# Adding arrays of sums in the order in which they are loaded, and skipping result rows that do not count

## The reference

```
h = tokens + attention(layernorm(tokens))
x = layernorm(h)                                   # 1184 x 256
topidx, tw = 6 of 32 experts for each token, with weights
routed = sum over the 6 chosen e of  tw[e] * down_e(silu(x @ gate_e) * (x @ up_e))
shared = silu(x @ shared_gate) * (x @ shared_up) @ shared_down
anchor = anchor_l(x)  with one of 16 small experts l, chosen by the first expert
return h + routed + shared + 0.1 * anchor
```

## Time and profile before

| what | value |
|---|---|
| median of 3 runs | 388.85 us |
| profiled execution | 390.52 us |
| its span | 388.7 us |
| TensorE busy | 350.9 us (90%) |
| VectorE busy | 256.1 us (66%) |
| GpSimd busy | 188.7 us (49%) |
| ScalarE busy | 168.9 us (43%) |
| moved by DMA | 86.62 MB, of it 25.51 MB by the software queue |
| read from HBM, written | 50.72 MB, 35.35 MB |

### The profile page before, as it was taken

How to read it: one execution, slowest core, us unless ns; L and a number is a source line. 1 busy time by engine, 2 the same in 40 slices (tenths; PEclk the granted TensorE clock), 3 DMA queues, 4 the chain that set the end, 5 groups by cost and what they waited for, 6 DMA issues and landing times.

```text
span 388.7 us, 8177 instructions
## 1 busy us (share of the span) xinstructions
PE 350.9 (90%) x2566; PEld 300.0 (77%) x2566; DVE 256.1 (66%) x1091; ACT 168.9 (43%) x433; POOL 188.7 (49%) x206
## 2 busy tenths in 40 slices
PE   5899999989999897776899999999999999997494
PEld 3687787968869777565689999999999999985231
DVE  3447588988979968588665555555555555555394
ACT  1124135253244522432166433347777777775001
POOL 5000000175572753723777777777665666655400
PEclk9899999999999989699999999999999999999879
DMA  7899998133159531349997776767788886499944
GB/s 232 245 356 329 284 422 365 47 103 103 60 159 389 191 106 31 119 119 406 317 268 234 225 215 205 210 205 216 208 239 247 253 239 209 141 312 332 309 131 130
DMA packets 39836, 86.62 MB, mean 223 GB/s; under 512 B 6513, under 2 KB 30185, under 8 KB 38745
## 3 DMA queue, kind: packets, MB, share of 16 engines
q1 hardware_dynamic: 29856, 59.84, 49.6%
q0 software_dynamic: 9072, 25.51, 19.0%
q10 hardware_dynamic: 864, 0.73, 0.7%
HBM read 50.72 MB, written 35.35 MB: 221 GB/s over the span
## 4 chain that ended last, share of the span: by engine, by line
PE 62%; DMA 15%; DVE 13%; ACT 4%; issue 2%; SPq 2%; DVEq 0%
PE B L854 19%; PE B L872 9%; DMA W<-sums_d 8%; PE B L545 5%; PE B L835 5%; PE B L580 4%; PE B L892 4%; DMA e_sb<-rows_d 4%; PE B L663 3%; DMA W<-in_wg 2%; PE B L629 2%; PE B L649 2%; DMA rows_d<-spent,slot 1%; PE B L687 1%; DVE stats L1083 1%
## 5 line engine op out<-in xcount | busy, mean ns | idle before, releaser
L508 POOL DMA_INDIRECT rows_d<-spent,slot x77 | 74.8, 972 | 124.9 <-DVE slot L1293 103.3
L529 POOL DMA_INDIRECT sums_d<-spent,to_row x60 | 58.3, 971 | 30.7 <-DVE spent L1534 24.0
L872 PE MATMUL B<-W,e_sb 128*128 (+1 forms) x224 | 67.8, 384 | 3.8 <-DVE e_sb L1542 3.6
L1542 DVE TENSOR_TENSOR e_sb<-e_sb,B 128x128 f32<-128x128 f32 (+1 forms) x112 | 32.2, 288 | 57.7 <-ACT e_sb L1036 56.7
L854 PEld LDWEIGHTS B<-e_sb,UPW 128*128 128x128 f32 x476 | 62.6, 191 | 4.2 <-issue 0.9
L854 PE MATMUL B<-e_sb,UPW 128*128 128x128 f32 x476 | 63.8, 275 | 0.0
L529 POOL DMA_INDIRECT sums_d<-Y_own,to_row x52 | 50.5, 972 | 21.2 <-DVE Y_own L1534 13.0
L1036 ACT ACTIVATE e_sb<-B 128x128 f32<-128x128 f32 (+1 forms) x112 | 30.9, 276 | 48.0 <-PE B L854 45.4
L854 PEld LDWEIGHTS B<-e_sb,W 128*128 128x128 f32 x320 | 43.1, 191 | 2.8 <-ACT e_sb L1031 0.5
L854 PE MATMUL B<-e_sb,W 128*128 128x128 f32 x320 | 43.6, 275 | 0.2 <-ACT e_sb L1031 0.2
L1031 ACT COPY e_sb<-B 128x256 f32<-128x256 f32 x112 | 41.2, 369 | 5.4 <-PE B L835 5.4
(11 more groups left out here) (193 smaller groups left out, 526.3 us busy)
## 6 DMA issues: line engine op xcount, KB each, us to landing
e_sb<-rows_d SPq DMA_DIRECT2D x96, 161.0 KB, 3.0
W<-sums_d SPq DMA_DIRECT2D x7, 1232.0 KB, 17.1
rows_d<-spent SPq DMA_DIRECT2D x1, 7728.0 KB, 33.8
W<-in_wx SPq DMA_DIRECT2D x1, 6643.0 KB, 48.9
W<-in_wx SPq DMA_DIRECT2D x10, 516.5 KB, 8.5
W<-in_wx SPq DMA_DIRECT2D x1, 4576.0 KB, 17.1
W<-in_pt SPq DMA_DIRECT2D x4, 666.0 KB, 7.2
spent<-rows_d SPq DMA_DIRECT2D x16, 161.0 KB
```

What stands on the lines that cost most here:

```text
L508: pool.indirect_dma_start(rows_d, bass.IndirectOffsetOnAxis(ap=slot[0:n, t, j:j + 1], axis=0), xrow[0:n, t, :], None).then_inc(done, 16)
L529: pool.indirect_dma_start(sums_d, bass.IndirectOffsetOnAxis(ap=to_row[:, i:i + 1], axis=0), result(i), None).then_inc(y_sent[i % NY], 16)
L872: pe.matmul(B[6 + i % 2][:, 0:D], hid[:, i % 2, :], weights, start=True, stop=True).then_inc(D_ps, 1)
L1542: dve.tensor_tensor(out[0:n, i % 2, :], S[0:n, i % 2, :], ups, ALU.mult).then_inc(H_ok, 1)
```

## The change

Two edits. The two adding engines take the seven arrays in the order 1, 2, ..., 6, 0, where they took 6, 5, ..., 0. And each send carries an upper bound for its row numbers, `SPARE_ROW - 1`; rows with a larger number are to be left out and not to be an error. The bound is passed in a register that is set ahead of every send.

```diff
+IN_ORDER = list(range(1, CHOICES)) + [0]
...
                 pool.indirect_dma_start(sums_d, bass.IndirectOffsetOnAxis(ap=to_row[:, i:i + 1], axis=0),
-                                        result(i), None).then_inc(y_sent[i % NY], 16)
+                                        result(i), None, bounds_check=SPARE_ROW - 1,
+                                        oob_is_err=False).then_inc(y_sent[i % NY], 16)
...
             pe.wait_ge(hs_ok, NB)
-            for c in range(CHOICES, -1, -1):
+            for c in [CHOICES] + IN_ORDER:
...
-            for c in range(CHOICES - 1, -1, -1):
+            for n, c in enumerate(IN_ORDER):
                 dve.wait_ge(fin_ld[c], 16)
                 for q, (lo, hi) in enumerate(ON_DVE):
-                    if c < CHOICES - 1:
-                        dve.wait_ge(fin_dve, len(ON_DVE) * (CHOICES - 2 - c) + q + 1)
+                    if n:
+                        dve.wait_ge(fin_dve, len(ON_DVE) * (n - 1) + q + 1)
```

## The result

The changed kernel takes **384.25 us** (median of 4 runs, 383.96 to 385.69), where the kernel before took 389.88 beside it: a ratio of **0.986 (95% interval 0.983 to 0.990)**, some 5.3 us less. (The ratios are taken over the fast runs of both kernels alone, and so are not quite the quotients of the medians.) A second measurement of the same kernel, further down, gave 0.989 (0.984 to 0.994). So the change makes the kernel faster, inside the range, but by half of the 10.6 us of the forecast. The profiled execution took 383.96 us, with a span of 382.2.

What follows compares the result with a forecast made beforehand. Adding waited for the sixth load, and sends held back by loads delayed the lists. Lists ending at 359.2, 14.1 us of adding, copy and stores gave a 378.1 span, 10.6 us less: 388.85 - 10.6 = 378.3 us, range 376.5 to 386.

Steps and rivals of the forecast that it cites:

- Rival A: Tail of the lists: bytes go, but a send's completion still waits behind the loads; 6.2 us less, 382.6; chance 0.12.
- rival B: Sends: skipped rows are not skipped on the wire, so the tail stays; 5.1 us less, 383.8; chance 0.08.
- Part 1, the order: Adding on both engines: starts when the lists end, not at the sixth load; VectorE 14.12 us, TensorE 13.9.
- What is late next: Loads after reordering: the sixth array is covered; the seventh lands 6.6 us after the last send lands.
- Part 2, the skipped rows: Sends beside the loads: skipping makes them land in 3.9 us, so the last weighing ends 4.5 us earlier.
- A second step: End of the sends: the last send starts at 360.7, lands at 364.6, and the seventh load at 371.2.
- The pace itself: Weighings of lists 103 to 108: 1.28 us apart, with bounds giving 1.6 us later to 2.5 earlier.
- Part 3, the bound: GpSimd's sends: register and index check taken as costing nothing; 0.09 us more per send would be free.
- hides there: Sends follow each other after 0.30 us with or without a wait instruction, so one more sequencer instruction costs nothing.
- rival C: GpSimd: the check makes it the bound; chance 0.14 with 0.15 to 0.28 us more per send, 0.08 beyond.

Runs made afterwards that it cites:

- One load at a time: Changed kernel with each of the six early loads issued only when the one before has landed: 391.07 us, ratio 1.004 to the kernel before.
- Freed weighings: Changed kernel without VectorE's wait for sends of the 14 lists (89 to 102) that hold no counted row: 385.31 us, ratio 0.988 to the kernel before.

## Why the prediction was half right

The time lies in the range only because the range also held the rivals A and B; the forecast's own sum had twice the gain.

**Part 1, the order: right in kind, too large in size.** The adding starts when the lists end, VectorE takes 14.11 us (14.12 said), TensorE does not idle and its clock stays at 1.00; its 1.88 + 10.46 + 1.97 us make 14.3 (13.9 said). Alone the order gives 3.1 us (1.9 to 4.4) where rival B's sum had 5.1. Of the other 2 us, 0.8 is a term that was sized too small, the end behind the seventh load: the forecast allowed 6.9 us from its landing to the end of the span, rival B 6.8; it takes 8.0 and 7.8 in the two profiles of after and 7.6 with the order alone. The last four matmuls take 1.97 for 1.7, and the last store, issued at 377.61 in the kernel after, goes out 0.8 us after the last copy's end and 4.5 us ahead of the end of the span, where 0.4 and 4.14 were taken over from the earlier trace rows. The rest is open; the one profile of the order alone has slower loads and a seventh array that is waited for 1.52 us, and does not say whether the order makes them slow. With both edits one loss is shown in the rows: VectorE's additions now run beside the last sends, and those take 1.22 and 1.70 us instead of 0.98, together 1.0 us in the path of the seventh load, which waits for every send. "What is late next" was asked of the loads and not of the sends.

**Part 2, the skipped rows: this step failed,** at the sentence that takes 3.9 us for the landing, "since these sends would carry almost nothing". The bytes are gone as said (6.17 MB); the landing of the empty sends is 9.0 to 11.5 us. The bounds, 2.4 and 10, were the right ones. The mistake was the row I took as nearest: the earlier trace rows has sends with their bytes and no loads beside them, at 2.4 to 5.4 us, and sends with their bytes and loads beside them, at 9.4 to 10.6. What sets these two groups apart is the loads, and the change took away none of these; I chose by the size of the send. One load at a time shows it directly, with 4.8 us. From there the errors follow in a row: the waits for sends stay, the last weighing ends at +29.1 instead of +22.6, the seventh load goes out at 367.77, +34.3, instead of +28.0.

The 2.0 us and the fixed price that the Trainium skill (DMA: Bandwidth & Descriptors, "Anatomy of one DMA — SWDGE (gpsimd) path") gives spoke against a gain by the skip, and so it came out, though for another reason than the skill's: its estimate of 2.3 us is near the 2.4 to 3.8 us of sends without loads beside them, and a fourth of what is measured beside the loads. The Trainium skill (DMA: Bandwidth & Descriptors, "Queues, rings and completion order") says that a transfer engine takes turns between its queues packet by packet. By that alone, and with packets as the profile counts them, a send's 48, an estimated three on each of 16 engines, would wait for about as many packets of the loads. A load has 112 such packets (one for each of 112 rows of 11 KB), seven for an engine, so an estimated 5.0 / 7 = 0.7 us each, and the send would land in an estimated 4 to 6 us: three of these and the 2.4 to 3.8 of a send alone. The 9 to 11.5 us with six loads queued do not agree, the 4.0 to 6.5 with one outstanding do.

**A second step would have failed if the first had held.** The forecast let the last send land 3.9 us after its issue. Freed weighings bring that issue to +25.4, before the loads end, and there it takes 7.82 us. TensorE, idle meanwhile, then has the granted clock of 0.50 and takes 3.76 us for the last array instead of the forecast's 1.7. The pace itself was sized well: weighed at +21.1, against +22.6 forecast with up to 2.5 earlier.

**Part 3, the bound: right for sends without a break, wrong beside the loads.** Without a break they are 1.284 us apart against 1.277, 0.98 long against 0.97; rival C did not come. But the sentence that one more instruction of the sequencer "hides there" was read from such sends only. In the tail GpSimd waits for the weighing, and there it does not hide: the weighing that ends at 348.91 is followed by the register's move, 0.03 us, and 0.71 us more until the send at 349.68, 0.77 in all; before, the one that ends at 342.75 was sent at 343.03, after 0.28. With the order alone it is 0.28 too, with the bound alone 0.78, so the bound makes the difference; whether its register or its check does is not told apart. Two such sends stand in the chain, each ahead of a weighing six lists later. That is 1.0 us on the way to the last weighing, which ends 2.0 us later than before (+29.1 against +27.1), a price that the forecast put at nothing.

**Rival A came about,** with a chance of 0.12: the bytes go, the completions still take their turn behind the loads. Its tail, 382.5 - 336.6 = 45.9, is met by 48.8 and 47.4. Of the 2.9 us that the first of these lacks, 2.0 lie in the weighings (on their way lie the bound's 1.0, and first waits of 2.46 us where it kept 0.60), 0.8 in the last sends and 1.1 behind the seventh load; the last send's landing (2.83 for 3.9) gives 1.1 back. Why the first sends beside the loads take 11.4 us here, when they take 8.9 at the least before and up to 13.2 with the order alone, is left open.

Nothing in the trace of before shows a small send beside loads, so that trace could not decide between 3.9 and 10 us. But its two groups of sends differ by the loads and not by their bytes, and that spoke for A more than the 0.12 that I gave it, against 0.58.

## What to carry to other kernels

When a cost has to be read from rows that differ in two things, sort them by what the change takes away and by what it leaves, and price the new case by what is left: here the loads beside it, not the bytes. A transfer beside several large loads got nothing from fewer bytes. What helped it was fewer loads outstanding, loads in pieces or fewer packets of its own, and only where the loads also went out earlier did the kernel get faster than the change: put the wait on the queue that needs the data, not on a compute engine that merely comes by. And when a wait is removed, look at what the freed engine then runs beside, and at where it waits instead: the last sends were slower beside the additions that start early, and where TensorE ran ahead to a late load, it had half its clock when the load came. A price that hides while an engine has a backlog (the bound's 0.5 us) need not hide where the engine waits.

## What the runs showed of the hardware

- A row that is skipped as out of bounds stays in its packet with 4 bytes: 9,072 packets before and after, 6.17 MB less, 1,497 more packets under 512 bytes. A send of 128 rows is 48 packets, of 16 rows 32.
- A send for which GpSimd waits starts 0.78 us after the end of its weighing with the bound (in the kernel after and with the bound alone) and 0.28 without it (before, and with the order alone); in sends without a break the difference is gone (1.284 against 1.277 us apart).
- A send that carries the bound and starts while VectorE adds takes GpSimd 1.22 to 1.74 us, 0.98 otherwise; so in after, and with the empty lists not waited for (1.40, 1.70, 1.70) or not sent (1.74, 1.70, 1.70). With the order alone the one send that starts beside the additions took 1.06, so what the bound has to do with it is open. The Trainium skill (SBUF — State Buffer, "SBUF: two separate sides") has VectorE and GpSimd share a pair of ports that an instruction holds to its end, also for a VectorE instruction with two inputs in SBUF against a GpSimd one that reads it. The rows with the bound agree in direction; the loss, 0.24 to 0.76 us, is less than one addition (14.11 / 14 = 1.01 us).
- The six loads of 1,232 KB land 5.0 us apart with full sends beside them (5.4 with the order alone), 5.0 and 4.5 with empty ones in the two profiles of after, and 4.8 with these left out: no difference clear of that between two executions.
- A send of 128 rows lands in 4.0 to 6.5 us with one load outstanding, and in 9 to 11.5 beside six queued at once (kernel after, until the last of them is nearly done: 5.2). Where sends crowd beside the six it is up to 14.9 (no wait for empty lists).
- The last four matmuls take 3.76 us at a granted clock of 0.50 where TensorE stood idle for 5.55 us ahead of them, and 1.97 us at 1.00 in the kernel after, where it was 0.22.
